# One scatter per step, and three small operations moved from VectorE to GpSimd, in a gated cross-attention and mixture-of-experts kernel

## What is computed

```python
x = x + tanh(g_xattn) * xattn(layernorm(x), ctx, ctx, W_qkv, b_qkv, W_out, b_out)   # 16 heads of 8
x = x + tanh(g_ffn)  * moe(layernorm(x), Wg, W1, b1, W2, b2)                        # 8 experts

def moe(x, Wg, W1, b1, W2, b2):            # tokens: 4096 x 128, C = 512
    gates = softmax(tokens @ Wg)
    idx = argmax(gates, axis=1)            # one expert per token
    locations1 = cumsum(one_hot(idx), axis=0) - 1      # its place there
    # kept where the place is < C; dispatch into (expert, place, feature)
    hidden = relu(expert_in @ W1 + b1)
    expert_out = hidden @ W2 + b2
    # out: each token's expert row times its gate
```

## Time and profile before

| | |
|---|---|
| runs, us | 344.57, 345.35, 347.14 (median 345.35) |
| the profiled execution's own time | 348.01 us |
| its span, first to last instruction | 346.2 us |
| mean granted TensorE clock | 0.834 |
| PE busy | 263.2 us (76%) |
| DVE busy | 215.3 us (62%) |
| POOL busy | 174.6 us (50%) |
| ACT busy | 150.9 us (44%) |

### The profile page before, as it was taken

One profiled execution on the slowest core, in us unless ns is written; L12 is line 12 of the kernel. 1 busy time (PEld: TensorE's weight loads), 2 busy tenths in 40 slices (PEclk: granted clock), 3 DMA queues, 4 the chain that ended last, 5 costly groups with the idle time before them and its releaser, 6 DMA issues.

```text
span 346.2 us, 8034 instructions
## 1 busy us (share of the span) xinstructions
PE 263.2 (76%) x2864; PEld 168.3 (49%) x2864; DVE 215.3 (62%) x718; ACT 150.9 (44%) x347; POOL 174.6 (50%) x202
## 2 busy tenths in 40 slices
PE   2557689897996996996996969959601999999910
PEld 1326446545544644544644536634301367777810
DVE  4768457699886896996875767954530144444520
ACT  4551563773773683773783443544200323222100
POOL 7509329139228828828728645043371005646472
PEclk9995578899699699899699695985855799999975
DMA  3726807806406316416315231016325315655310
GB/s 105 209 85 198 231 4 235 247 11 200 131 15 184 112 47 183 117 44 184 89 39 156 68 122 31 5 62 154 86 69 150 92 31 152 210 156 170 84 43 21
DMA packets 50919, 39.25 MB, mean 113 GB/s; under 512 B 9698, under 2 KB 47223, under 8 KB 50880
## 3 DMA queue, kind: packets, MB, share of 16 engines
q1 hardware_dynamic: 47168, 28.67, 30.1%
q0 software_dynamic: 3712, 10.07, 9.0%
HBM read 13.72 MB, written 12.65 MB: 76 GB/s over the span
## 4 chain that ended last, share of the span: by engine, by line
PE 43%; issue 17%; DVE 10%; ACT 8%; POOL 8%; another core or an unknown queue 5%; DMA 4%; POOLq 1%; SPq 0%; ACTq 0%; DVEq 0%
PE O L496 10%; PE S L465 6%; POOL out_dram L1125 5%; PE TS L480 5%; PE M L528 4%; DVE negm L757 3%; ACT prob L643 3%; PE X L427 2%; DVE nm L818 2%; PE X L440 2%; PE X L521 2%; PE TS L581 2%; DMA qp<-mrow 2%; PE X L433 1%
## 5 line engine op out<-in xcount | busy, mean ns | idle before, releaser
L757 DVE TENSOR_REDUCE negm<-S 128x4 f32<-128x512 f32 x128 | 82.4, 683 | 31.1 <-PE S L465 17.7
L643 ACT ACTIVATE prob<-TS 128x512 f32<-128x512 f32 x128 | 72.2, 589 | 58.8 <-PE TS L480 42.9
L496 PE MATMUL O<-prob,vals 128*32 128x128 f32 x1024 | 61.2, 316 | 4.7 <-issue 3.8
L260 POOL TENSOR_TENSOR rest_k<-full_k,parts_k 128x512 f32<-128x512 f32 x7 | 8.1, 1154 | 69.6 <-ACT parts_k L626 69.6
L465 PE MATMUL S<-kp,qp 62*128 62x128 bf16 x512 | 32.8, 244 | 7.8 <-DVE negm L757 7.5
L480 PE MATMUL TS<-qp,kp 64*128 64x128 bf16 x512 | 33.1, 246 | 7.2 <-ACT prob L643 4.0
L1066 POOL DMA_INDIRECT rec_dram<-rec,slot x32 | 31.9, 998 | 10.1 <-issue 10.1
L1125 POOL DMA_INDIRECT out_dram<-fin,tok x32 | 31.3, 979 | 11.2 <-issue 11.2
L496 PEld LDWEIGHTS O<-prob,vals 128*32 128x32 f32 x1024 | 22.2, 116 | 30.0 <-issue 15.4
L465 PEld LDWEIGHTS S<-kp,qp 62*128 62x128 bf16 x512 | 19.1, 104 | 25.0 <-issue 15.6
L1035 POOL TENSOR_TENSOR fence_p<-pool_c 128x1 f32<-128x1 f32 x16 | 3.1, 194 | 54.2 <-DVE fin L1015 34.4
(11 more groups left out here) (132 smaller groups left out, 495.9 us busy)
## 6 DMA issues: line engine op xcount, KB each, us to landing
kp<-parts_k SPq DMA_DIRECT2D x48, 128.0 KB
qp<-parts_q SPq DMA_DIRECT2D x48, 128.0 KB, 2.5
rec_dram<-zeros POOLq DMA_DIRECT2D x8, 516.0 KB
xr<-rec_dram SPq DMA_DIRECT2D x8, 260.0 KB
x_sb<-in_x_dram SPq DMA_DIRECT2D x8, 256.0 KB, 3.6
c_sb<-in_ctx_dram SPq DMA_DIRECT2D x8, 256.0 KB, 3.6
out_dram<-rec SPq DMA_DIRECT2D x8, 256.0 KB
w1s<-in_L_ffn_W_dram SPq DMA_DIRECT2D x8, 256.0 KB
```

Source lines behind the costliest of these rows:

```text
L496: mm = nc.tensor.matmul(o_out[i * HV:(i + 1) * HV, u * L:(u + 1) * L], vals[G % 2][:, k, h, :], prob[n % 2][:, h * L:(h + 1) * L], start=( ...
L643: nc.scalar.activation(prob[n % 2][:, first:first + 4 * L], TS[:, a, :], ACT.Exp).then_inc(a_exp, 1)
L757: V.tensor_reduce(negm[n % 2][:, first:first + 4], S[:, a, :].rearrange("p (h k) -> p h k", k=L), AX.X, ALU.max, negate=True).then_inc(v_r ...
```

## The change

Four edits. (1) `scatter` takes a batch number k: a group's first row scatter stays at j = 3, the other three go to the ends of the next three steps (each behind `pool.wait_ge(v_x1, c - 4)`); of the last but one group two go at j = 2 and two at j = 3 of steps 34 and 35, and the last group's four stay together. (2) `offset1` leaves VectorE. A new `statistics1` on GpSimd makes the negated mean `neg1`, the root, `nm1` and `sd1`, at j = 0 where the root was. (3) `scaled` goes from VectorE to GpSimd, at j = 1 before the split of q. (4) `fence` on VectorE is a maximum over four columns of one input where it was a product of two.

```diff
-            def offset1(H):
-                dve.wait_ge(g_rs1, H + 1)
-                V.scalar_tensor_tensor(nm1[:], mv1[:, :, 0], -1.0, rs1[:, 1, :], ALU.mult, ALU.mult).then_inc(v_nm, 1)
-                V.tensor_tensor(sd1[H % 2][:], rs1[:, 0, :], rs1[:, 1, :], ALU.mult).then_inc(v_sd, 1)
...
-                return V.tensor_tensor(fence_v[:, i:i + 1], ident[:, 0:1], ident[:, 0:1], ALU.mult)
+                return V.tensor_reduce(fence_v[:, i:i + 1], ident[:, 0:4], AX.X, ALU.max)
...
+            def statistics1(H):
+                pool.wait_ge(v_mv1, H + 1)
+                if H >= 1:
+                    pool.wait_ge(a_xn, H)
+                    pool.wait_ge(g_sd, H)
+                G_.tensor_tensor(neg1[:], mv1[:, :, 0], pool_c[:, 2, :], ALU.mult).then_inc(g_neg, 1)
+                root(H, mv1, rs1, v_mv1, g_e1).then_inc(g_rs1, 1)
+                pool.wait_ge(g_neg, H + 1)
+                pool.wait_ge(g_rs1, H + 1)
+                G_.tensor_tensor(nm1[:], neg1[:], rs1[:, 1, :], ALU.mult).then_inc(g_nm, 1)
+                if H >= 2:
+                    pool.wait_ge(v_xl, H - 1)
+                G_.tensor_tensor(sd1[H % 2][:], rs1[:, 0, :], rs1[:, 1, :], ALU.mult).then_inc(g_sd, 1)
...
+            def scaled(G):
+                pool.wait_ge(v_lraw, G + 1)
+                pool.wait_ge(g_rs2, G + 1)
+                G_.tensor_tensor(ldif[:], ldif[:], rs2[:, 1, :].unsqueeze(2).broadcast_to([P, GB, E]), ALU.mult).then_inc(g_ldif, 1)
...
-                for k in range(GB):
-                    G_.indirect_dma_start(rec_dram, bass.IndirectOffsetOnAxis(slot[p][:, k:k + 1], 0), rec[p][:, k, 0:REC], None,
-                                          bounds_check=T - 1, oob_is_err=False).then_inc(sent[p], 16)
+                G_.indirect_dma_start(rec_dram, bass.IndirectOffsetOnAxis(slot[p][:, k:k + 1], 0), rec[p][:, k, 0:REC], None,
+                                      bounds_check=T - 1, oob_is_err=False).then_inc(sent[p], 16)
...
-                if j == 3 and is_group(g - 2):
-                    scatter(g - 2)
+                if j < 3 and is_group(g - 3) and g - 3 < NG - 2:
+                    pool.wait_ge(v_x1, min(c - 4, B))
+                    scatter(g - 3, j + 1)
+                if j >= 2 and g - 2 == NG - 2:
+                    for k in range(GB // 2):
+                        scatter(NG - 2, (j - 2) * (GB // 2) + k)
+                elif j == 3 and g - 2 == NG - 1:
+                    for k in range(GB):
+                        scatter(NG - 1, k)
+                elif j == 3 and is_group(g - 2):
+                    scatter(g - 2, 0)
```

More of the change, by code:

```diff
@@ L117, in flamingo_kernel @@
         rs1 = sb("rs1", [P, 2, GB])
+        neg1 = sb("neg1", [P, GB])
         nm1 = sb("nm1", [P, GB])
@@ L1053, in norm2, with scatter @@
                 G_.tensor_tensor(to, to, rs2[:, 1, :].unsqueeze(2).broadcast_to(spread), ALU.mult).then_inc(g_xn2, 1)
-            def scatter(G):
+            def scatter(G, k):
                 p = G % 3
[L1057 to L1064, removed]
-                for k in range(GB):
-                    G_.indirect_dma_start(rec_dram, bass.IndirectOffsetOnAxis(slot[p][:, k:k + 1], 0), rec[p][:, k, 0:REC], None,
-                                          bounds_check=T - 1, oob_is_err=False).then_inc(sent[p], 16)
+                if k == 0:
+                    if G == 0:
+                        for q in range(3):
+                            pool.wait_ge(sent[q], zeros_sent(q))
+                    pool.wait_ge(g_xn2, G + 1)
+                    pool.wait_ge(v_slot, G + 1)
+                    if G == NG - 1:
+                        pool.wait_ge(g_fence, NG - 1)
+                    fence()
+                G_.indirect_dma_start(rec_dram, bass.IndirectOffsetOnAxis(slot[p][:, k:k + 1], 0), rec[p][:, k, 0:REC], None,
+                                      bounds_check=T - 1, oob_is_err=False).then_inc(sent[p], 16)
             def step(c):
@@ L1071, in step @@
                 if j == 0 and is_group(g + 2) and g + 2 >= 2:
-                    root(g + 2, mv1, rs1, v_mv1, g_e1).then_inc(g_rs1, 1)
+                    statistics1(g + 2)
                 if j == 0 and is_group(g - 2):
@@ L1081, in step @@
                     zero_records(i)
+                if j == 1 and is_group(g - 2):
+                    scaled(g - 2)
                 if j == 1 and is_group(g + 1) and g + 1 != 0:
@@ L1103, in _ @@
             G_.memset(pool_c[:, 0, :], EPS)
+            G_.memset(pool_c[:, 2, :], -1.0)
             G_.memset(pool_c[:, 1, :], -0.5).then_inc(s_pset, 1)
```

29 lines of the change are left out of this document (9 added, 20 removed).

## The result

The changed kernel takes **318.55 us** (median of 4 runs, 317.38 to 320.49) beside 346.25 us (4 runs, 344.57 to 349.43) for the kernel before: ratio 0.9196, 95% interval 0.9111 to 0.928. That is 27.7 us less, where 20 were forecast; the range was 315 to 338. In a later comparison the same kernel stood at 321.65 against 347.36 us, ratio 0.9272 (0.9197 to 0.9348). Of most kernels here some executions take over 1.5% longer than the quickest; the ratios leave these out, the medians don't. The profiled span fell from 346.2 to 318.7 us.

What follows compares the result with a forecast made beforehand. Bound: a relay between TensorE, ScalarE and VectorE, held by runs of scatters and VectorE's stalls against GpSimd. 28 + 7 removed, 6 + 6 + 2 + 1.1 added: 345.35 - 20 gives 325 us, range 315 to 338.

Steps and rivals of the forecast that it cites:

- The six runs: Loop's six runs of four scatters: spreading them removes hold and slow clock, 4.7 us each, 28 us.
- Lone scatters: Steps 11 to 34: 24 single scatters, each delaying TensorE's news by 0.25 us, 6 us added.
- each its price: Rival: a scatter costs the same wherever it stands, 24 singles at 0.8 us, 338 us in all; chance 0.16.
- nm and sd: Moved to GpSimd, ending VectorE's stalls beside its large operations: 8 us less 1 us, net 7 us removed.
- ldif late: Steps 13, 17, 21: product queued on GpSimd makes `lexp` some 1.5 us late; with slow clock 6 us added.
- 0.4 us of slow clock: Steps 13, 17, 21: TensorE's clock loss charged with each late product, within 3 x 1.9 = 6 us.
- Other two-input work: VectorE's `route` and `place` may now fall on GpSimd's large operations: 2 us added, bounds 0 to 8.
- The tail: Last group: product behind norm2's large operations on GpSimd, last scatters' fence at 257.0 instead of 255.91 us: 1.1 us lost.
- step 9's `ldif`: Product on VectorE held by a GpSimd addition in step 9: 1.2 us removed by moving it.
- 340 us: Rival: the holds have nothing to do with scatters, perhaps busy DMA engines, so all six stay; chance 0.08.

Runs made afterwards that it cites:

- e5: Kernel before with every slot moved beyond the bound, so scatters are issued but no record is written: 347.12 us, ratio 0.9975.
- e6: Kernel before with plain transfers of the same records to consecutive rows in place of the 32 indirect scatters: 316.88 us, ratio 0.9134.
- e8: Changed kernel with the scatters of groups 0 to 5 in pairs, two at j = 3 and two at j = 1: 324.83 us, ratio 0.9273.
- e9: Kernel before with one 128x4 power on GpSimd between one scatter and the next of groups 0 to 6: 343.84 us, ratio 0.993.
- e3: Changed kernel with only the logits' product (ldif) back on VectorE, behind the score maxima: 318.83 us, ratio 0.9227.
- e4: Changed kernel with only nm and sd back on VectorE: 327.8 us, ratio 0.9485.
- e1: Kernel before with only the scatters spread one per step; nm, sd, product and fences stay on VectorE: 333.42 us, ratio 0.9629.
- e11: Changed kernel with GpSimd reordered: no scatter between norm2 and product, one ahead of k's split; last group's product ahead of norm2's large operations: 324.73 us.
- e12: e11 with x's addition on GpSimd also held until the older group's slots are made: 331.02 us, ratio 0.9575.

## Why the forecast was right in sign and 7.7 us short

- **The six runs, 28 us removed.** Right. The mechanism is shown by e5, e6, e8 and e9 together: indirect scatters with gaps of 0.3 us delay the news of TensorE's finished work; not the data, not the number in some ten us. The sum is right too: e6 wins 10.5 + 17.4 = 27.9 us in the two middle stretches. In that was luck: I took 4.7 us for every run from the pair around step 13, and they cost 3.5 us each up to slot 3 and 5.8 behind it.
- **Lone scatters, 6 us added.** Too high. After takes 58.1 us from slot 3 to 6 and e6 55.0, with 12 lone scatters between them: 3.1 / 12 = 0.26 us each if nothing else differs. e3 (product on VectorE, as in e6) is 2.6 us above e6 in both stretches, with 24: 0.11 us each. The rival "each its price", 0.8 us each, is out.
- **nm and sd, net 7 us.** Right: 94.9 to 87.5 is 7.4 us at slot 0, and e4, which undoes it alone, stands at 94.2. But on top of e1, with the product still on VectorE, the same move and the fences won 14.6 us (e3), so this price holds only with the product on GpSimd.
- **ldif late, 6 us added.** The waits came as forecast, three of up to 1.9 us, and e3 prices the stretch at 5.2 to 5.7 us. But e11 removed these waits and won nothing, so that price isn't shown to be the lateness's: in e3 the copy's collision was smaller as well (2.9 instead of 7.9 us by line), and the clock held. The 0.4 us of slow clock that I charged three times didn't come.
- **Other two-input work, 2 us.** The copy in `place` collides, median 0.77 and at most 1.96 us, where I had one class and a guess; in return `cand` at step 28 is free again. Its net price stays open between these two.
- **The tail, 1.1 us lost.** Right: slot 6 to 7 takes 10.6 us, 0.9 more than before, and the last scatters' fence stands at 227.79 us, 28.1 us earlier than in rows 12, where slot 6 is 29.1 earlier. What I missed is that the same lateness splits a run of seven scatters (e1: 4.94, e3: 5.62 us of hold).

**Where the 7.7 us lie.** By stretches the change won 7.4 (forecast 7), 7.3 (forecast 3 x 4.7 - 3 - 6 - 1, some 4), 14.3 (forecast 3 x 4.7 - 3 - 1, some 10), and lost 0.9 and 0.6 behind. So all of it lies in the two middle stretches, and since e6 wins there what I took for the runs, it lies in what I added: 6 + 6 + 2 = 14 us. The changed kernel needs 129.4 us for the two stretches and e6 123.1, so 6.3 us were added. By e3 (125.7), 2.6 us came with the spread and the other edits and 3.7 with the product on GpSimd; this split rests on one execution each. One term I had put at nothing without a reason: only step 9's `ldif` was counted as removed. Once the holds are gone it matters in later steps too: in e6 it is on the chain of waits with 1.12 us at 109.55 and at 131.85 us.

The form of the sum was wrong as well: I added the terms as if each were worth the same whatever the others do. By e1 the spread alone wins 12.9 us, not 22, since the product then falls on the split of q and the tail gets a hold. By e3 the move of `nm` and `sd` takes the product's collision away as the product's own move does. That the sum came out within the range is in part because the change makes all the moves at once.

The Trainium skill's rule that I had set against the change (SBUF — State Buffer, "Who interferes with whom": TensorE and ScalarE never wait on anyone, only VectorE and GpSimd contend) holds for the port, as e4's 2.22 and 2.74 us show once more. For the news of TensorE's work, reading it so gave 340 us, and e9 speaks against that reading: the same scatters with and without gaps, and the waits behind TensorE's finished work are there or gone.

## What to carry to other kernels

Don't issue indirect transfers from GpSimd back to back while a relay of small steps runs; more than a microsecond of other GpSimd work between two of them is enough, but use work that has to be done anyway, since a gap of idle work came back as lateness (e9). When a fix shortens an engine's queue, ask what that engine's large operations will now stand beside: `nm`, `sd` and the fences, moved with the product left on VectorE, won 14.6 us on top of the spread scatters, while all the moved operations together won 6.5 us without the spread. A zero from undoing an edit (e3) can be the sum of large terms; cut the span in stretches before calling it nothing.

## What the runs showed of the hardware

- Four indirect scatters 0.30 us apart put TensorE's and ScalarE's relay on hold for 2.4 + 1.8 us, seven for 4.9 to 5.6 us; with 1.2 to 1.3 us between them (e9), none. Of twelve pairs 0.30 us apart three show an unknown wait (e8: 2.0, 2.1 and 0.4 us). Dropping all records changes nothing (2.43 + 1.82 us), and four plain transfers back to back (2.17 us) hold nothing at a DMA share of 0.83.
- A power on 128x4 costs GpSimd 1.06 us, five times an addition of that shape (0.21 us). Small operations of VectorE that ran beside GpSimd's 128x512 and 128x544 operations took up to 2.74 us in the rows shown.
- TensorE's granted clock stayed 1.00 over three windows of 25 us with 22 us of work in each (after), and was 0.84 to 0.87 in e11 and e12 with 21.8 to 23.5 us of busy time a window. What made it fall there no run resolves.
